# A recommender tower on one core: the last layer's result in another bank, and its place beside the next tile's first layer

## What is computed

```python
# e: (1024, 32, 16) gathered from 32 tables by ids
x0 = e; xk = x0; outs = []
for W in (W0, W1, W2):                       # W0 (32,32,64), W1 and W2 (32,64,64)
    xk = relu(einsum('bmd,bhd,mhk->bkd', x0, xk, W))
    outs.append(sum(xk, axis=2))             # over the 16 dimensions
h = concatenate(outs + [dense_ctx], axis=1)  # 192 + 16 columns
h = maximum(h @ W_top1 + b_top1, 0)          # 208 -> 512
h = maximum(h @ W_top2 + b_top2, 0)          # 512 -> 256
y = h @ W_top3                               # 256 -> 1
```

## Time and profile before

| | us |
|---|---|
| device time, median of 3 executions | 613.0 |
| lowest and highest of the 3 | 612.41, 613.72 |
| the profiled execution's own time | 612.51 |
| its span in the trace | 610.7 |
| outside the span (612.51 - 610.7) | 1.8 |
| TensorE busy in the span | 558.8 (92%) |
| VectorE busy | 550.1 (90%) |
| GpSimd busy | 451.7 (74%) |
| ScalarE busy | 407.2 (67%) |
| mean granted TensorE clock | 0.994 of full speed |

### The profile page before, as it was taken

The page is one execution under the profiler, slowest core; times in us unless marked ns, Lnnn a source line. Parts: engine busy times, 40 slices in busy tenths (PEclk is TensorE's granted clock), DMA queues, the critical chain, the costliest instruction groups (busy, mean ns, idle before and its releaser), DMA issues.

```text
span 610.7 us, 9346 instructions
## 1 busy us (share of the span) xinstructions
PE 558.8 (92%) x2656; PEld 198.9 (33%) x2656; DVE 550.1 (90%) x269; ACT 407.2 (67%) x2720; POOL 451.7 (74%) x347
## 2 busy tenths in 40 slices
PE   0048889999999999999999999999999999999997
PEld 0012222323334343333334343333334333333334
DVE  0068799999999999999999999999999999999991
ACT  0030706677867688778867688677867688768852
POOL 6748888878988878888888889888887884214640
PEclk9998999999999999999999999999999999999999
DMA  5297979793598819894598819894597919891000
GB/s 168 69 386 249 389 240 397 252 400 122 173 398 294 325 38 370 285 396 172 188 387 295 319 46 383 291 375 169 164 399 271 353 37 380 292 413 68 2 1 2
DMA packets 54119, 152.04 MB, mean 249 GB/s; under 512 B 9681, under 2 KB 18769, under 8 KB 54066
## 3 DMA queue, kind: packets, MB, share of 16 engines
q1 hardware_dynamic: 45874, 149.32, 65.3%
q0 software_dynamic: 8192, 2.11, 2.9%
HBM read 147.20 MB, written 4.20 MB: 248 GB/s over the span
## 4 chain that ended last, share of the span: by engine, by line
PE 73%; DVE 11%; issue 5%; POOL 5%; DMA 4%; SPq 1%; ACT 1%; DVEq 0%; POOLq 0%
PE acc L620 67%; DVE zd L420 10%; POOL emb L328 4%; DMA rolled<-x_scratch 3%; PE mlp L651 2%; PE acc L629 1%; PE mlp L642 1%; PE mlp L643 1%; SPq L293 1%; POOL zg L340 1%; PE mlp L658 1%; ACT xk_sb L496 0%; DMA emb<-tables_in,index 0%; ACT xk_ps L496 0%; DMA ids_sb<-ids_in 0%
## 5 line engine op out<-in xcount | busy, mean ns | idle before, releaser
L420 DVE TENSOR_TENSOR zd<-rolled,xk_ps 128x2048 f32<-128x2048 f32 (+1 forms) x246 | 535.4, 2248 | 13.0 <-DMA rolled<-x_scratch 7.8
L620 PE MATMUL acc<-zd,w_sb 128*64 128x512 f32 x1700 | 390.1, 598 | 9.0 <-DVE zd L420 8.9
L328 POOL DMA_INDIRECT emb<-tables_in,index x256 | 244.4, 955 | 78.5 <-issue 65.2
L340 POOL TENSOR_TENSOR zg<-rolled,xk_sb 128x1024 f32<-128x1024 f32 x87 | 207.1, 2383 | 56.5 <-ACT xk_sb L496 41.4
L620 PEld LDWEIGHTS acc<-zd,w_sb 128*64 128x64 f32 x1700 | 119.6, 138 | 258.4 <-issue 218.6
L475 ACT ACTIVATE relu_ab<-acc 128x16 f32<-128x16 f32 x1152 | 190.8, 302 | 3.8 <-PE acc L620 3.5
L475 ACT ACTIVATION_READ_ACCUMULATOR relu_ab<-acc 128x1 f32 x1152 | 191.6, 329 | 0.1
L496 ACT ACTIVATE xk_sb<-acc 64x512 f32<-64x512 f32 x128 | 76.4, 597 | 55.8 <-PE acc L620 53.3
L620 PE MATMUL acc<-zd,w 128*64 128x512 f32 x256 | 61.9, 603 | 37.4 <-DVE zd L420 37.4
L620 PE MATMUL acc<-zg,w_sb 128*64 128x512 f32 x348 | 90.5, 599 | 2.3 <-POOL zg L340 2.3
L496 ACT ACTIVATE xk_ps<-acc 64x512 f32<-64x512 f32 x126 | 71.8, 570 | 29.6 <-PE acc L620 26.7
(11 more groups left out here) (42 smaller groups left out, 89.7 us busy)
## 6 DMA issues: line engine op xcount, KB each, us to landing
rolled<-x_scratch SPq DMA_DIRECT2D x256, 512.0 KB, 9.9
base<-x_scratch SPq DMA_DIRECT2D x16, 512.0 KB
emb<-tables_in,index POOLq DMA_INDIRECT x256
x_scratch<-emb SPq DMA_DIRECT2D x32, 128.0 KB
w_sb<-w_in SPq DMA_DIRECT2D x2, 512.0 KB, 4.9
wt<-wtop_in SPq DMA_DIRECT2D x1, 512.0 KB, 6.9
wt1a<-wtop_in SPq DMA_DIRECT2D x1, 256.0 KB, 5.6
w<-w0a_in SPq DMA_DIRECT2D x1, 160.0 KB, 2.4
```

Source lines behind the costliest of these rows:

```text
L328: pool.indirect_dma_start(emb[:, i % 2, c * DIM:(c + 1) * DIM], None, tables, bass.IndirectOffsetOnAxis(index[:, g:g + 1].bitcast(U32), 0) ...
L340: nc.gpsimd.tensor_tensor(zg[:, n % ZG_BUFS, :], rolled[:, s, j, :], xk_sb[:, s, :], ALU.mult).then_inc(zg_ready, 1)
L420: nc.vector.tensor_tensor(zd[:, n % ZD_BUFS, 0:w, :], rolled[:, s, j:j + w, :], repeated(layer_in, w), ALU.mult).then_inc(zd_ready, 1)
L620: end = nc.tensor.matmul(acc[h * MAPS:(h + 1) * MAPS, bank, :], weights, z[:, h * HALF:(h + 1) * HALF], start=(j + c == 0), stop=(i == len ...
```

## The change

mlp3's result moves from the bank `mlp` to columns 256 to 383 of partition 0 of `stage`. mlp3 of tile m-1 moves from behind item 4 of phase (a, 1, 1) to behind item 2 of phase (b, 1, 0), and mlp1 of tile m follows right on it (before: behind item 3 of that phase). ScalarE's `y_to_sb(m - 1)` moves from ahead of `sum_d(b, 0)` to behind `h1_to_sb(m)`. The waits change with it: mlp1 waits for h2 (that mlp2's results are out of the bank) in place of `y_ready`; mlp3 waits until `sum_d(b, 0)` has read `stage`, and until the result before is copied out; the first layer of every even stream from 6 on waits for the copy of the result that lay in `stage`. For the last mlp3 of the loop (tile 6, in phase 62) only the bank and the waits change, not its place.

```diff
-        y_bank = mlp[0:1, 2 * TB:3 * TB]
+        y_bank = stage[0:1, 2 * TB:3 * TB]
@@ ScalarE
                 zsum_to_sb(m)
-                if m > 0:
-                    y_to_sb(m - 1)
                 sum_d(b, 0)
                 evacuate(a, 1)
                 h1_to_sb(m)
+                if m > 0:
+                    y_to_sb(m - 1)
                 sum_d(a, 1)
@@ TensorE, phase
+                if layer == 0 and stream % 2 == 0 and stream >= 6:
+                    pe.wait_ge(y_ready, stream // 2 - 2)
@@ mlp1
                 if m > 0:
-                    pe.wait_ge(y_ready, m)
+                    pe.wait_ge(h2_sb, 2 * m)
@@ mlp3
             def mlp3(m):
+                pe.wait_ge(summed, act_sums_to(min(2 * m + 5, STREAMS - 1), 0))
+                if m > 0:
+                    pe.wait_ge(y_ready, m)
                 pe.wait_ge(h2_sb, 2 * (m + 1))
@@ the loop over tiles
-                phase(q + 5, {4: lambda: mlp3(m - 1)} if m > 0 else {})
-                phase(q + 6, {3: lambda: mlp1(m)})
+                phase(q + 5)
+                def result_and_layer_1():
+                    if m > 0:
+                        mlp3(m - 1)
+                    mlp1(m)
+                phase(q + 6, {2: result_and_layer_1})
```

## The result

The changed kernel takes 614.5 us (median of 18 executions, 612.28 to 619.91), the kernel before 612.9 beside it (18 executions, 610.94 to 614.31): 1.0038 times as long, 95% interval 1.002 to 1.0056. So it is slower by 1.7 us, where 0.6 us faster was forecast. The profiled execution is a bad one even for this kernel: 618.65 us, with a span of 616.9.

What follows compares the result with a forecast made beforehand. TensorE was taken to bound the kernel, VectorE 0.73 us behind. Four tiles at -0.30 and two late ones at +0.32 gave -0.6 us, from a median of 613.0 to 612.4; the 8-in-10 range was 611.0 to 614.0.

Steps and rivals of the forecast that it cites:

- What bounds the kernel: Steady tiles: TensorE sets the period of 68.49 us, and VectorE is 0.73 us from setting it.
- The rule of the lag: Item 2 of (b, 1, 0): VectorE lateness d costs max(0, d - 0.62) us before the change, all of d after.
- Part 1: mlp3 at its old place costs 0.68 us, some 0.24 of it entering and leaving; mlp1 costs 2.13.
- Part 2: mlp3 right ahead of mlp1 costs 0.32 us, sharing the switch and covering mlp1's first load; TensorE saves 0.36 a tile.
- Rival 2: Switch or first load not saved beside mlp1: mlp3 costs 0.44 to 0.56, total 613.2 to 613.9 us; chance 0.15.
- Part 3: At item 2 of (b, 1, 0), 0.06 us goes to waiting for VectorE: free tiles gain 0.30, late ones lose at most 0.32.
- Part 4: Effects on ScalarE, GpSimd, SyncE and waits: worth 0; the change moves neither end of the `rolled` wait that makes VectorE late.
- Cover for mlp3's new wait: Behind item 2 of (b, 1, 0), `sum_d(b, 0)` ends 3.6 us before TensorE gets to mlp3.
- Rival 3: VectorE sets item 2's start in most tiles; lateness over 0.30 loses up to 0.32 a tile, 614.9 us at most; chance 0.14.
- Rival 4: ScalarE's wait at `y_to_sb` was on the path: 11 us would go, to 602; chance 0.01.
- the step from the spread of the executions to d: Executions of the kernel before spread by 1.3 us, as they would if VectorE's lateness varies.
- The signs I had named: In TensorE's trace: mlp3 plus mlp1 about 2.45 us, free tiles 68.2, VectorE's wait about 0.4, late tiles 0.3 longer.

Runs made afterwards that it cites:

- before_again: The kernel before with no edit, run again for a second trace, on the third chip: 1.0002 times the kernel before.
- before_third: The kernel before with no edit, run once more beside the changed kernel on the fifth chip: 1.0004 times the kernel before.
- pair_item1: Against the changed kernel, mlp3 and mlp1 one item earlier, behind item 1 of phase (b, 1, 0): 610.0 us, 0.9974 times the kernel before.
- pair_item1_third: The kernel with mlp3 and mlp1 behind item 1 of (b, 1, 0), unedited, on one more chip: 612.9 us, 0.9999 times the kernel before.
- the doses: One extra small VectorE product behind item 1 of odd streams' first layers, in both kernels: 1.0048 (kernel before) and 1.0068 (changed kernel).
- before_w64: Against the kernel before, mlp3's weights padded with zeros to 64 columns, nothing moved: 610.7 us, 0.998 times the kernel before.
- pair_item0: Against the changed kernel, mlp3 and mlp1 two items earlier, behind item 0 of (b, 1, 0): 614.4 us, 1.0054 times the kernel before.
- the light kernels: Both kernels with chunks 8 to 15 of `rolled` loaded for a quarter of their columns: 611.2 us (kernel before) and 611.7 us (changed kernel).
- after_fifth: The changed kernel with no edit, run again on the fifth chip: 615.53 us, 1.004 times the kernel before.

## Why the prediction was wrong

In short: the sum took mlp3 beside mlp1 at 0.32 us, and it costs 0.53, because going from 1 output column to 128 has a price of its own. With that the saving no longer covers what the lost lag costs in a late tile, and the profiled execution had far more lateness than the forecast assumed. The parts one by one:

**What bounds the kernel: right. The rule of the lag: right for lateness that arises behind phase (a, 1, 0).** The undisturbed tiles of every run stand where TensorE's pace puts them, but for the 0.11 at item 2. The rule said max(0, d - 0.62) before and all of d after:

| kernel | d | tile | over the free tile |
|---|---|---|---|
| before_again | 1.02 | 68.96 | 0.47 |
| before_third | 1.25 | 69.18 | 0.69 |
| before (its trace) | 1.37 | 69.29 | 0.80 |
| before_third, d at the last item of (a, 1, 0) | 0.53 | 69.03 | 0.54 |
| after (its trace) | 0.29 | 68.75 | 0.30 |
| after (its trace) | 1.11 | 69.61 | 1.16 |
| after (its trace) | 2.22 | 70.68 | 2.23 |
| pair_item1 | 0.51 | 68.50 | 0.16 |
| pair_item1_third | 1.62 | 69.61 | 1.27 |

What before gets for nothing is 0.55 to 0.57 (0.60 by the doses) in place of 0.62. The pair behind item 1 gets 0.35.

The row of before_third with 0.53 breaks the rule, and shows what the prediction had overlooked: item 2 of (b, 1, 0) isn't the only tight point of a tile. VectorE's product for the last item of (a, 1, 0) is ready 0.07 us before TensorE takes it, in the kernel before and in the changed one. In a free tile of before it is the second of these two, ready at 257.91 + 4.47 = 262.38, and TensorE's eight records for it, the last eight of the row here, begin at 262.46:

```profile
257.91 4.47 DVE L420 TENSOR_TENSOR zd<-rolled,xk_ps 128x2048 f32<-128x2048 f32 x2
```

```profile
262.03 2.35 PE L620 MATMUL acc<-zd,w_sb 128*64 128x512 f32 x10
```

So lateness up to this item costs nearly all of itself in either kernel (0.54 of 0.53 in before_third; 68.52 with d = 0.21 in before_w64, whose free tile is 68.25), and the 0.6 of the kernel before pays only for what arises between it and item 2. The loads' waits and the stalls in (a, 1, 1) do, so the sums below hold.

**Part 1: right.** mlp3 costs 0.68 where it stands and mlp1 2.13; before_w64 takes 0.24 off the tile by making the widths equal, which is the 0.24 of entering and leaving.

**Part 2: the step that failed, a term of the sum that was mis-sized.** mlp3 costs 0.53 beside mlp1, not 0.32, so TensorE saves 0.15 and not 0.36. The step held that the chunks' half width was what mlp3 and mlp1 both differ from, and so that they share one mode. They don't: one column and 128 columns differ as well. It also held that mlp1's first weight load would be covered; its first record was as slow as before. Rival 2 had this, at 0.44 to 0.56. My evidence for the saving, the pace of 0.11 in the flow, was from records of one width; a trace of before with mlp3 and mlp1 side by side didn't exist, and the bound nearest to what was unknown deserved more than 0.15. The Trainium skill's sentence on row groups, which the prediction set aside, doesn't give the size either: by it mlp3 would have cost 0.44.

**Part 3: 0.06 lost to VectorE was 0.11.** Free tile: -0.04 instead of -0.30, of which 0.21 is part 2 and 0.05 this. Those 0.26 us, in the four free tiles and as much or a little less in the two late ones, are 1.5 of the 2.3 us between the forecast's -0.6 and the measured +1.7.

**Part 4: lateness was taken to be the same in both kernels, and in the traces of three chips of five it wasn't.** With the rule and the terms as measured, and the lateness of the trace of before (d = 1.37 and 0.64 in two tiles), the changed kernel would have paid 2.01 for it where before paid 0.88 (69.29 and 68.57 against 68.49), and 6 x 0.04 = 0.24 less for the rest: +0.9 us, 613.4 by the profiled execution. So the mis-sized terms alone turn the forecast's -0.6 into +0.9. The two chips without late counts measured +0.2 and +0.5 us, in intervals that hold 0. The profiled execution had 6.9 us of lateness over six tiles instead of 2.0. By before's rule the same d would have cost 4.2 (0.57, 1.63 and 2.05 in the three worst tiles), so of the 5.8 us in the steady part some 3.4 (4.2 - 0.9) are lateness that the trace of before didn't have, and 2.4 the lag that was gone (6.9 - 4.2), less the 0.24. The prediction looked for lateness only in the loads and took two tiles of one trace as its size. It was blind to the late counts because the trace of before shows none. That they make up the remaining 0.8 us of the median is argued from the one traced execution.

**Cover for mlp3's new wait: right**, 3.6 us behind item 2; pair_item0 found its end.

**Rival 3** named the mechanism that decided, d over 0.30 in most tiles with no lag left, but bounded it at +0.32 a tile, as if d were the same in both kernels. Rival 4 is out: nothing of ScalarE's 1.81 us was gained anywhere. And the step from the spread of the executions to d doesn't hold: the light kernels spread by 2.7 and 3.5 us with no d in the traced execution.

**The signs I had named** came out so: the pair 2.66 us (wrong from 2.57), free tiles 68.45 (wrong if 68.3 isn't reached), VectorE's wait 0.68 and not 0.4, a late tile longer than before's by 0.56 for the same d, where 0.3 was named.

**What stays open.** Why the counts come late in some traces, whether this goes with the chip, and why the changed order is stopped by them so much more. In it `evacuate(a, 1)` ends 2 us sooner, and GpSimd's gathers begin earlier against VectorE: the six gathers beside (a, 1, 1) start 42.0 us behind VectorE's first item of (a, 2, 0) in two tiles of after_fifth, and 42.8, 43.6 and 43.4 in three of before_third. In the traces with late counts no tile in which they start at 42.8 or later has a stall in (a, 1, 1), and the one tile of before_third in which they start at 42.0 has its stall one phase earlier. But of the tiles with 42.5 or less some have a stall and some have none. So the gathers' place may be the cause and isn't shown to be. A kernel that moves the gathers alone wasn't tried.

## What to carry to other kernels

A small matmul whose output width differs from its neighbours' costs by the change of width: give it theirs (here 64 columns, 63 of them zeros, 0.24 us a tile) before moving it. When a step leaves the stretch ahead of a hand-over, the engine behind it comes earlier and the lag that had absorbed lateness is gone: read how large it is at every item and not at one, and put the step at a point where it stays (here one item earlier, 0.997 in place of 1.0004 on the same chip). And ask what lateness the next trace could have, rather than take that of a single one.

## What the hardware showed that I had not expected

- Matmuls with 1 and with 128 output columns, one behind the other: 0.20 us to the next start and 0.21 to the one after, where 0.11 is the pace; gone with equal widths. Between 64 columns and 64 nothing at all.
- A count of TensorE for which VectorE starts 0.9 to 3.0 us behind the item's end, in six of the twenty traces and only in tiles in which GpSimd issues gathers; in thirteen traces the count rises 0.02 us behind that end. The one left, before_again, has the incomplete record of the six and no such stall.
- The same VectorE product on 128x320 numbers took 0.48 us four times, and 0.83, 1.34 and 1.61 in other tiles of the same execution. Why wasn't tested.
